# Reciprocal square roots by a power and one Newton step on GpSimd, in place of VectorE guesses and three steps

## What is computed

```python
h = tok(x)                                   # (32, 313, 128)
h = h + attn(layernorm(h))                   # softmax(z z^T) z, per clip
h = h + ffn(layernorm(h), Wq, bq, ln_g, ln_b, keys0, keys1, down, up)

# ffn, per row, for 8 heads of 64 columns:
q = (hs @ Wq.T + bq).reshape(b, s, 8, 64)
q = (q - mu) / sqrt(var + 1e-5) * ln_g + ln_b
s0 = l2norm(q[..., :32]) @ l2norm(keys0).T   # 64 scores
s1 = l2norm(q[..., 32:]) @ l2norm(keys1).T
sc0, ix0 = top_k(s0, 16); sc1, ix1 = top_k(s1, 16)
fs, pos = top_k(all 256 sums sc0[i] + sc1[j], 16)
fi = (ix0[i] + ix1[j]) at pos; w = softmax(fs)
out = sum over heads and picks of gelu(hs . down[fi]) * w * up[fi]
```

## Time and profile before

| | us |
|---|---|
| median of three runs | 2026.2 (2025.46 to 2030.39) |
| the profiled execution, its own time | 2031.43 |
| its span, first to last instruction | 2029.6 |
| DVE busy | 1919.0 (95%), 15718 instructions |
| PE busy | 1632.5 (80%) |
| POOL busy | 1433.2 (71%), 2561 instructions |
| ACT busy | 1232.0 (61%) |

### The profile page before, as it was taken

How to read it: one execution, slowest core, us unless ns; L and a number is a source line. 1 busy time by engine, 2 the same in 40 slices (tenths; PEclk the granted TensorE clock), 3 DMA queues, 4 the chain that set the end, 5 groups by cost and what they waited for, 6 DMA issues and landing times.

```text
span 2029.6 us, 47236 instructions
## 1 busy us (share of the span) xinstructions
PE 1632.5 (80%) x11023; PEld 1169.5 (58%) x11023; DVE 1919.0 (95%) x15718; ACT 1232.0 (61%) x3883; POOL 1433.2 (71%) x2561
## 2 busy tenths in 40 slices
PE   5577888788888888888888788888878888986667
PEld 3235566566656655665666556656656565655456
DVE  2499999999999999999999999999999999999992
ACT  3346666666666666566556766656675665665554
POOL 2247777686777767777776777777687777767775
PEclk8877888888888787888888787888888888788765
DMA  1000000000000000000000000000000000000000
GB/s 44 7 10 4 19 7 13 13 7 19 7 19 9 13 13 6 19 7 19 7 6 22 6 19 7 19 7 7 19 9 20 7 19 7 6 13 9 7 6 11
DMA packets 46669, 24.87 MB, mean 12 GB/s; under 512 B 4827, under 2 KB 46116, under 8 KB 46390
## 3 DMA queue, kind: packets, MB, share of 16 engines
q1 hardware_dynamic: 46390, 21.85, 3.9%
HBM read 11.58 MB, written 10.26 MB: 11 GB/s over the span
## 4 chain that ended last, share of the span: by engine, by line
DVE 79%; PE 11%; ACT 5%; issue 4%; POOL 1%; SPq 1%; DMA 0%; DVEq 0%; ACTq 0%
DVE idx L1071 11%; DVE idx L1078 11%; DVE hrest L1065 10%; DVE alpha L1039 10%; DVE vals L1069 7%; DVE vals L1062 7%; DVE c L1109 5%; DVE crest L1103 5%; DVE top L1106 3%; DVE top L1100 3%; PE QB L526 2%; DVE beta L1044 2%; PE FB L418 1%; PE QB L514 1%; DVE lo L1033 1%
## 5 line engine op out<-in xcount | busy, mean ns | idle before, releaser
L914 POOL TENSOR_TENSOR bw<-beta,wp 128x1024 bf16<-128x1024 bf16 x240 | 505.2, 2135 | 347.3 <-issue 171.6
L526 PE MATMUL QB<-bw,alpha 128*128 128x48 bf16 x5120 | 554.5, 277 | 106.7 <-issue 101.1
L526 PEld LDWEIGHTS QB<-bw,alpha 128*128 128x128 bf16 x5120 | 521.0, 150 | 149.2 <-issue 139.4
L749 ACT ACTIVATE WD<-QB 32x96 f32<-32x96 f32 x1280 | 307.6, 240 | 84.5 <-PE QB L526 71.6
L1039 DVE TENSOR_SCALAR alpha<-hi 128x1024 bf16<-128x1024 bf16 x640 | 274.9, 502 | 0.0
L475 PE MATMUL SC<-WK,hidT 128*128 128x512 f32 x320 | 241.0, 846 | 12.6 <-issue 11.8
L1071 DVE FIND_INDEX8 idx<-vals,sraw 128x8 uint32<-128x64 f32 x1280 | 250.6, 218 | 0.0
L1078 DVE FIND_INDEX8 idx<-vals,hrest 128x8 uint32<-128x64 f32 x1280 | 250.6, 219 | 0.0
L1065 DVE MATCH_REPLACE8 hrest<-vals,sraw 128x64 f32<-128x64 f32 x1280 | 249.6, 207 | 0.0
L1062 DVE MAX8 vals<-sraw 128x8 f32<-128x64 f32 x1280 | 169.1, 207 | 14.1 <-ACT sraw L729 14.1
L1069 DVE MAX8 vals<-hrest 128x8 f32<-128x64 f32 x1280 | 166.6, 208 | 0.0
(11 more groups left out here) (206 smaller groups left out, 3583.3 us busy)
## 6 DMA issues: line engine op xcount, KB each, us to landing
res<-h_scratch SPq DMA_DIRECT2D x80, 64.0 KB, 1.9
xin<-in_x SPq DMA_DIRECT2D x32, 128.0 KB
h_scratch<-h2n SPq DMA_DIRECT2D x32, 128.0 KB
out<-ofin SPq DMA_DIRECT2D x64, 64.0 KB, 1.5
h_scratch<-h2n SPq DMA_DIRECT2D x32, 28.5 KB
out<-ofin SPq DMA_DIRECT2D x16, 57.0 KB
xin<-in_x SPq DMA_DIRECT2D x32, 28.0 KB
xin<-in_x SPq DMA_DIRECT2D x32, 0.2 KB
```

The lines of the kernel that those rows point to most:

```text
L526: last = mm(bank[:, 48 * u:48 * u + 48], alpha[:, buf, a, :, 8 * p + u], bwv[:, :, a, :, 8 * p + u], start=(a == 0), stop=(a == 1))
L749: last = A(WD[r, RING[(t - 4) % NT], :, 8 * p:8 * p + 8], blocks[r, :, :, g], ACT.Copy)
L914: last = tt(bw[:, buf, NY * i:NY * i + NY, :], beta[:, buf, :, :], wp[:, buf, i, :].unsqueeze(1).to_broadcast([128, NY, 256]), ALU.mult)
```

## The change

DVE makes no guesses any more. POOL computes the reciprocal square root itself: an elementwise power with exponent -0.5 and one Newton step on it, five operations for twelve. The Newton step is p * (3 - p * p * x4) with x4 = 4x and p = x4 ** -0.5, so that half of the result needs no further factor; each quantity is therefore formed four times as large. For the variances DVE writes a second copy `u3` = 4 v3, and `nA`, `nB`, `C2` and the floor of the norms carry the factor in instructions that were there, except one added in the set-up (`C2`). The scaled row sums of the layer norms, `sv`, are formed on POOL in two operations. POOL waits for the sums (`ss1_full`, `ss2_full`), the variances (`v3_full`) or the norms (`n2_steps`) in place of the guesses, and `half_norms` gets a wait for `stat_full`.

```diff
-            def newton(y, xh, a, c, sem_, base, end=None):
-
-                i = 0
-                for r in range(3):
-                    for o, p0, p1, op in ((a, y, y, ALU.mult), (a, a, xh, ALU.mult), (a, a, c, ALU.add), (end if end is not None and r == 2 else y, y, a, ALU.mult)):
-                        if i:
-                            pool.wait_ge(sem_, base + i)
-                        tt(o, p0, p1, op).then_inc(sem_, 1)
-                        i += 1
+            def rsqrt(out_, x4, p, a, n, sem_, base):
+
+                rows_ = out_.shape[0]
+                c_half, c_3 = chalf[0:rows_, 0:n], c3[0:rows_, 0:n]
+                tt(p, x4, c_half, ALU.pow).then_inc(sem_, 1)
+                pool.wait_ge(sem_, base + 1)
+                tt(a, p, p, ALU.mult).then_inc(sem_, 1)
+                pool.wait_ge(sem_, base + 2)
+                tt(a, a, x4, ALU.mult).then_inc(sem_, 1)
+                pool.wait_ge(sem_, base + 3)
+                tt(a, c_3, a, ALU.subtract).then_inc(sem_, 1)
+                pool.wait_ge(sem_, base + 4)
+                tt(out_, p, a, ALU.mult).then_inc(sem_, 1)
+
+            def row_rsqrt(i, j, sem_):
+
+                tt(sv[i][:], ss[i][:], cmean[:], ALU.mult).then_inc(sem_, 1)
+                pool.wait_ge(sem_, 7 * j + 1)
+                tt(sv[i][:], sv[i][:], ceps[:], ALU.add).then_inc(sem_, 1)
+                pool.wait_ge(sem_, 7 * j + 2)
+                rsqrt(sy[i][:], sv[i][:], sxh[i][:], sa[:, 0:6], 6, sem_, 7 * j + 2)
...
             def front(j, t, p):
                 if (t, p) == (0, 2):
-                    pool.wait_ge(s["seed1_full"], j + 1)
-                    newton(sy[0][:], sxh[0][:], sa[:, 0:6], c15[:, 0:6], s["newton1"], 12 * j)
+                    pool.wait_ge(s["ss1_full"], 2 * j + 2)
+                    row_rsqrt(0, j, s["newton1"])
                 if (t, p) == (2, 0):
-                    pool.wait_ge(s["seed2_full"], j + 1)
-                    newton(sy[1][:], sxh[1][:], sa[:, 0:6], c15[:, 0:6], s["newton2"], 12 * j)
+                    pool.wait_ge(s["ss2_full"], 2 * j + 2)
+                    row_rsqrt(1, j, s["newton2"])
                 if (t, p) == (3, 3):
-                    pool.wait_ge(s["seed3_full"], j + 1)
-                    newton(y3[:], xh3[:], sa[:], c15[:, 0:40], s["newton3"], 12 * j)
-                    pool.wait_ge(s["newton3"], 12 * j + 12)
+                    pool.wait_ge(s["v3_full"], j + 1)
+                    rsqrt(y3[:], u3[:], xh3[:], sa[:], 40, s["newton3"], 5 * j)
+                    pool.wait_ge(s["newton3"], 5 * j + 5)
                     tt(std[:], v3[:], y3[:], ALU.mult).then_inc(s["std_steps"], 1)
...
+                pool.wait_ge(s["stat_full"], j + 1)
                 tt(halves(nB[:]), halves(nB[:]), both(std[:]), ALU.mult).then_inc(s["nrm_steps"], 1)
...
                 if p == 0 and t == 1 and exists(k, t, 0):
-                    pool.wait_ge(s["seed4_full"], k + 1)
-                    newton(y4[:], xh4[:], na[:], c15[:], s["rn_steps"], 12 * k, rn[:])
+                    pool.wait_ge(s["n2_steps"], 2 * k + 2)
+                    rsqrt(rn[:], n2[:], xh4[:], na[:], 80, s["rn_steps"], 5 * k)
...
-            def row_seed(i, j, done):
-
-                dve.wait_ge((s["ss1_full"], s["ss2_full"])[i], 2 * j + 2)
-                V.tensor_scalar(sv[i][:], ss[i][:], 1.0 / D, 1e-5, ALU.mult, ALU.add).then_inc((s["sv1"], s["sv2"])[i], 1)
-                dve.wait_ge((s["sv1"], s["sv2"])[i], j + 1)
-                seed(sv[i][:], sxh[i][:], sy[i][:], done)
-
...
-                if (t, p) == (2, 1):
-                    row_seed(1, j, s["seed2_full"])
                 if (t, p) == (3, 3):
                     bank = f_wait(dve, "VAR", j)
                     stat = bank[:, 0:40 * NT].rearrange("p (t n) -> p t n", t=NT)
+                    V.tensor_scalar(u3[:].rearrange("p (t h) -> p t h", t=NT), stat[:, :, 0:H], 4.0, 4e-5, ALU.mult, ALU.add)
                     V.tensor_scalar(v3[:].rearrange("p (t h) -> p t h", t=NT), stat[:, :, 0:H], 1e-5, None, ALU.add
                                     ).then_inc(s["v3_full"], 1)
-                    V.tensor_copy(nA[:].rearrange("p (t n) -> p t n", t=NT), stat[:, :, 8:24])
+                    V.tensor_scalar(nA[:].rearrange("p (t n) -> p t n", t=NT), stat[:, :, 8:24], 4.0, None, ALU.mult)
...
-                    dve.wait_ge(s["v3_full"], j + 1)
-                    seed(v3[:], xh3[:], y3[:], s["seed3_full"])
...
-                dve.wait_ge(s["n2_steps"], 2 * j + 2)
-                seed(n2[:], xh4[:], y4[:], s["seed4_full"])
...
                         if t == 0:
                             norms(k)
-                            if k + 1 < PAIRS:
-                                row_seed(0, k + 1, s["seed1_full"])
```

More of the change, by code:

```diff
@@ L9 @@
 BF16 = mybir.dt.bfloat16
-I32 = mybir.dt.int32
 U32 = mybir.dt.uint32
@@ L38 @@
 BASE = 768.0
-RSQRT_MAGIC = float(0x5F3759DF)
 RING = [0, 1, 0, 1, 2]
@@ L105, in build @@
         cdig = sb("cdig", [128, NS])
-        c15 = sb("c15", [128, 80])
+        c3 = sb("c3", [128, 80])
+        chalf = sb("chalf", [128, 80])
+        cmean = sb("cmean", [128, 6])
+        ceps = sb("ceps", [128, 6])
         WcT = sb("WcT", [128, 512])
@@ L148, in build @@
         v3 = sb("v3", [128, 40])
+        u3 = sb("u3", [128, 40])
         xh3 = sb("xh3", [128, 40])
@@ L161, in build @@
         xh4 = sb("xh4", [128, 80])
-        y4 = sb("y4", [128, 80])
         na = sb("na", [128, 80])
@@ L237, in build @@
         names = """loaded head_loaded xin_zeroed zeroed wqT_full bmean_full wmean_full wcT_full bqc_in_full gbq_full bm_half bqT_full kss_part
-            kseed_full knewton kn_full kbT_full dT_full weights_ready x_full xT_copied ss1_full sv1 seed1_full
-            newton1 xn_full xnT_copied e_full rden_full h2c_full ss2_full sv2 seed2_full newton2 h2_full
-            hid_full hidTn_full sq_full v3_full seed3_full newton3 std_full stdT_full hidT_full
+            knewton kn_full kbT_full dT_full weights_ready x_full xT_copied ss1_full
+            newton1 xn_full xnT_copied e_full rden_full h2c_full ss2_full newton2 h2_full
+            hid_full hidTn_full sq_full v3_full newton3 std_full stdT_full hidT_full
             inner_full gelu_full gl_full hcs_full scores_full sraw_full eb_full
@@ L245, in build @@
             top_chain cand_chain identb_full wgn_psum wgn_full wk_psum wk_full bk_steps bks_psum bks_full
-            wb_steps stat_full vt_full std_steps nrm_steps n2_steps seed4_full""".split()
+            wb_steps stat_full vt_full std_steps nrm_steps n2_steps """.split()
         s = {n: sem(n) for n in names}
@@ L622, in front @@
                 if (t, p) == (0, 2):
-                    act.wait_ge(s["newton1"], 12 * j + 12)
+                    act.wait_ge(s["newton1"], 7 * j + 7)
                     act.wait_ge(s["hcs_full"], 2 * j + 2)
@@ L650, in front @@
                 if (t, p) == (2, 1):
-                    act.wait_ge(s["newton2"], 12 * j + 12)
+                    act.wait_ge(s["newton2"], 7 * j + 7)
                     for b in range(2):
@@ L786, in setup @@
                 nc.gpsimd.memset(ss[1][:], 1.0)
-                nc.gpsimd.memset(c15[:], 1.5)
+                nc.gpsimd.memset(c3[:], 3.0)
+                nc.gpsimd.memset(chalf[:], -0.5)
+                nc.gpsimd.memset(cmean[:], 4.0 / D)
+                nc.gpsimd.memset(ceps[:], 4e-5)
                 nc.gpsimd.memset(one[:], 1.0)
@@ L883, in slot @@
                     kk, t1 = (k, t - 1) if t else (k - 1, NT - 1)
-                    pool.wait_ge(s["rn_steps"], 12 * kk + 12)
+                    pool.wait_ge(s["rn_steps"], 5 * kk + 5)
                     after(pool, s["cs_full"], n - 1)
@@ L924, in _ @@
             V = nc.vector
-            def seed(x_, xh, y, done):
-                V.tensor_scalar(xh, x_, -0.5, None, ALU.mult)
-                V.tensor_scalar(y.bitcast(I32), x_.bitcast(I32), -0.5, RSQRT_MAGIC, ALU.mult, ALU.add).then_inc(done, 1)
             def heads(ap, n=QD):
@@ L941, in setup @@
                 dve.wait_ge(s["kss_part"], 2)
-                V.tensor_scalar(kss[:], kss[:], 1e-24, None, ALU.max).then_inc(s["kss_part"], 1)
-                dve.wait_ge(s["kss_part"], 3)
-                seed(kss[:], kxh[:], ky[:], s["kseed_full"])
+                V.tensor_scalar(kss[:], kss[:], 1e-24, 4.0, ALU.max, ALU.mult).then_inc(s["kss_part"], 1)
                 V.tensor_reduce(bmean[:], heads(bqB[:]), AX.X, ALU.add).then_inc(s["bmean_full"], 1)
@@ L971, in setup @@
                                 ALU.mult).then_inc(s["weights_ready"], 1)
-                dve.wait_ge(s["knewton"], 12)
+                dve.wait_ge(s["knewton"], 5)
                 for i in range(4):
@@ L1004, in front @@
                     stat = bank[:, 0:40 * NT].rearrange("p (t n) -> p t n", t=NT)
+                    V.tensor_scalar(u3[:].rearrange("p (t h) -> p t h", t=NT), stat[:, :, 0:H], 4.0, 4e-5, ALU.mult, ALU.add)
```

(12 more changed lines are left out.)

8 lines of the change are left out of this document (3 added, 5 removed).

## The result

The changed kernel takes 2191.0 us (2188.3 to 2192.5, four runs) against 2025.8 in the same comparison: ratio 1.081, 95% interval 1.080 to 1.082, so 165 us slower. Forecast were 1987 us and a range of 1968 to 2040. It went as rival (a) has it, at a price beyond the one that I had set as its end.

What follows compares the result with a forecast made beforehand. Bound: a loop of DVE (24.0 us), PE and ACT (71.0), POOL (24.4). Savings 8.9 + 14 x 1.42 + 1.6 + 0.9 + 4.5 + 1.8 = 37.6, plus 1.6, total 39 us: 1992 profiled, 1987 median; range 1968 to 2040.

Steps and rivals of the forecast that it cites:

- rival (a): Power is dear and POOL takes DVE's place: slower, about 2079 us at 100 ns a column; chance 17%.
- the price of the power: On POOL, 25 ns a column: 1.0 us more than a multiply for 40 columns, 2.0 for 80; upper bound 100 ns.
- The model of the loop: One pair of 119.4 us is 24.0 us on DVE, 71.0 on PE and ACT, 24.4 on POOL.
- 0.58 us from DVE's leg: Five DVE instructions go at t0 between the two passes of indices, saving 0.58 us a pair.
- 2.42 from POOL's: Variances on POOL after `bw` of t3: seven operations fewer at 0.346 us, power priced as a multiply, 2.42 us a pair.
- the second leg: PE and ACT's stretch from `beta` of t0 to `bw` of t3, 71.0 us, claimed to stay and cover the norms' savings.
- B: Length from end of `beta` at t0 to start of `bw` of t3, forecast to stay at 71 us.
- Nothing waits for them in the steady pairs: POOL's row sums, twelve operations of 0.2 us becoming seven, are under cover in steady pairs.
- stand still while a POOL operation runs: DVE's SBUF compares wait inside their own time for POOL: eight `alpha` take 2.76 us at t0, 5.44 at t4.
- still 4 to 5: Sign of being right: `alpha` at t4 still takes 4 to 5 us, at t1 2.8.
- 4.5 + 1.8 us and 1.6 of the first pair: Head savings: key norms and first row roots 4.5 us, first pair's variances 1.8, DVE instructions at t2 and t3 1.6.
- The Trainium skill's 6 us for a first call: First call to freshly loaded POOL code might cost about 6 us in the head, ending the kernel 6 us later.

Runs made afterwards that it cites:

- the runs with two Newton steps: Kernel before with two Newton steps on POOL instead of three, 2005.7 us; the same with guesses of row sums and norms, and row means, on POOL, 1983.1 us.
- all but norms: Changed kernel with the 80 norms done the old way; row sums, keys and the 40 variances use the power; 2074.9 us.
- the rows alone: Changed kernel with the power for row sums and keys only, variances and norms the old way; 2026.3 us.
- the run cut in five: Changed kernel with variances the old way and the norms' five operations split into 16 columns per tile, ahead of `vs`; 2133.3 us.
- the cheap operation: Changed kernel with a multiply in the place of the power, same operations, order and waits, output not the reference's; 1973.4 us.
- the price list: Kernel before with multiplies and powers of several sizes and values appended behind the end of POOL's program; 2135 us in its one run.
- the kernel with the norms' power ahead of `bw`: Changed kernel with variances the old way and the norms' power split ahead of `bw`: 16 columns at t0, t1, t2, 32 at t3; 2027.6 us.

## Why the prediction was wrong

**The step that failed is the price of the power.** It stood at 25 ns a column, with an end of 100, reasoned from what elementary operations would make a root. Measured are 160 ns a column and 0.4 us. "Against it: it would have to cost some 36 elementary operations a column" is where the 17% came from; it costs 76 of the 2.1 ns that I used as unit. An end of four times one's own guess isn't a bound from a row, and the range built on it shut out the case that came.

**The model of the loop held.** With the power as cheap as a multiply the text's own terms give 1987 - 15 = 1972 us; 1973.4 was measured. Term by term: 0.58 us from DVE's leg, measured 0.74; 2.42 from POOL's, measured 2.5; the second leg stays at 71.0, measured 71.0. One term was held for the wrong thing all the same: B of 69 us in the runs with two Newton steps shows that 71 isn't PE's and ACT's own length.

**Rival (a) named both places.** Its rule for the variances, the leg grows one for one, makes 6.5 us at the true price, less 2.4 for the seven operations, 4.1 a pair; all but norms shows 3.1 more than the rows alone (122.4 against 119.3). For the norms, what goes beyond the start of `bw` of t1: at 100 ns it said 2.4 us, at the true 13.8 us dearer the same slack gives 8.2, and B grew by 7.5. The rival then should have been weighed by how little was known of its price. What it missed is that both together cost 15 to 18 us more.

**The cover.** "Nothing waits for them in the steady pairs" and "norms ... under the second leg" were argued from idle time of POOL, and idle time turned out to have a place in the list: the run cut in five fell over the same point.

**The lock waiting.** DVE's SBUF compares "stand still while a POOL operation runs" doesn't hold for the power: `alpha` takes 2.77 us inside it at t1, as forecast for that row but for another reason. At t4 "still 4 to 5" holds at the price forecast (4.82 with the cheap operation, median), but not in the change: also 2.77, and POOL waits in its place.

**The head.** 4.5 + 1.8 us and 1.6 of the first pair were to go, with 1.0 more at the price of a multiply: 8.9. With the cheap operation `beta` of the first t0 ends at 189.9 us, 10.7 earlier than before; with the change at 205.0, 4.4 later. The power in the rows alone gives 197.9, and 204.3 with the variances' added, so 6.4 us are the 40-column power (6.76 us), which is in the open there.

**The Trainium skill's 6 us for a first call** (GPSIMD Engine Reference, Instruction dispatch) don't show: the first power of the change, 64x2, takes 745 ns and starts at 15.5 us, where POOL's first root operation stood before. The first of the price list starts 0.08 us behind the multiply ahead of it and takes 1.34 us, as those of its size in the change do (1336 ns on the mean).

## What to carry to other kernels

An operation that no row prices needs a run of its own before it goes on a serial leg; eight known operations given up for one unknown are a bet on that one. Idle time of an in-order engine is usable only at its place in the list: put long work directly ahead of the instruction that waits, behind all that others wait for. When two engines hold each other up inside their instructions, making one earlier can move the wait to the other, and only the timeline of both tells.

## What the runs showed of the hardware

- POOL's elementwise power costs 160 ns a column, in 1 partition as in 128, whatever the two values of the pairs tried; a multiply of 128x40 beside it is 0.27 us.
- It doesn't hold DVE's SBUF compares up: eight `alpha` take 2.77 us inside it, as they do at t3 where no power runs. But it doesn't end before them. In the change and in the kernel with the norms' power ahead of `bw`, each norms' power that had `alpha` beside it (15 and 58 of them) ends 0.05 to 0.2 us behind the last `beta`, whatever its length: 14.18 us instead of 13.14 at 80 columns, and at 16 columns, alone 2.92, it takes 3.90 at t0, 3.29 at t2 and this at t1 (POOL and then DVE):

```profile
1528.55 6.09 POOL L791 TENSOR_TENSOR xh<-n,chalf 128x16 f32<-128x16 f32 x1
```

```profile
1531.28 2.76 DVE L1062 TENSOR_SCALAR alpha<-hi 128x1024 bf16<-128x1024 bf16 x8
1533.96 0.62 DVE L1067 TENSOR_SCALAR beta<-lo 128x256 bf16<-128x256 bf16 x4
```

- POOL's copy to bf16 that starts 0.13 us behind `alpha` takes 3.48 us instead of 0.44, 0.3 us past the end of `beta`: in the earlier trace rows it was DVE that waited in this tile, behind POOL operations that had started first.
